# Earlier output copy, earlier first values and a score ring that runs across four heads

## The chip, the cores and the metric

The kernel runs on one core of one Trainium2 chip. The metric is the device time of one execution in microseconds (us); less is better. Three executions of the kernel before took 1312.82, 1315.09 and 1315.27 us.

## The reference

The input x is four sequences of 1024 tokens with 128 features, float32. Three residual steps follow each other, each on a layer-normalised x: half of a mixture-of-experts feed-forward, attention, and half of the same feed-forward again.

```
x = x + 0.5 * ffn(layernorm(x))          # 8 experts of width 256, top 2, silu gate
x = x + attention(layernorm(x))
x = x + 0.5 * ffn(layernorm(x))

attention: qkv = x @ qkv_w + qkv_b; 16 heads of 8; rotary on q and k
           weights = softmax(q @ k.T * 8**-0.5); out = (weights @ v) @ out_w + out_b
```

Batch times heads gives 64 independent heads, each with a score matrix of 1024 by 1024. This change touches only the attention over these heads.

## The kernel before, in words

All engines run hand-written instruction streams that meet at semaphores. The feed-forward stages are left as they are. The heads are handled one after the other, in a loop whose body holds four heads (u = 0 to 3), with the first four and the last four heads written out.

The scores of one head are computed twice on TensorE. Once with queries on the partitions, so that VectorE can take each query's maximum (`max_scores`, L866, and the reduction at L1243); and once with keys on the partitions, so that ScalarE can exponentiate them (`key_scores`, L895, and L662) and TensorE can multiply the exponentials with the values (`weigh_values`, L908). The maximum is split into three bf16 parts on GpSimd (L503 to L509), transposed on TensorE (`max_transpose`, L885), copied to SBUF by ScalarE (`mrow_copy`, L642) and brought by DMA (L360) into three extra rows of the query operand, so that the second score product comes out with the maximum already subtracted.

TensorE's order within head n is a loop over i = 0 to 15. In step i it issues one key-score matmul of head n (512 columns) and one max-score matmul of head n+2 (512 columns). After an odd i it issues one block of values: eight recorded matmuls for one block kb of 128 keys. Values run LAG = 2 blocks behind the scores, so after i = 1 and i = 3 the last two blocks (6 and 7) of head n-1 are done, and after i = 7, 9, 11, 13, 15 the blocks 1 to 5 of head n. Block 0 of head n stands after i = FIRST_VALUES = 6. The transposition of head n+1's maxima stands before i = MT_AT = 7. The values of a head add up in PSUM bank 7, which ScalarE copies out (`o_copy`, L650) after the exponential i = 3 of the next head; the copy waits until values block 7 is done, and values block 0 of the next head waits for the copy.

PSUM is cut thus: banks 0 to 2 are a ring for key scores and the transposed maxima; banks 3 to 6 are two pairs for the max scores; bank 7 holds the values' sum. A place of the ring is one bank in turn (place modulo 3). The ring has 18 places per head: sixteen scores, the transposition at place 7, and place 17, which is left empty so that the next head starts at bank 0 again. `place_before` names the work that used the same bank before, and `bank_free` makes TensorE wait for its reader on ScalarE. A max-score pair t (i = 2t and 2t+1) waits until VectorE has read pair t-2 (L865).

SyncE's queue issues, per head: the loads of Q and K of head n+3 (L353), the store of the copied output (L366) and the load of the maxima's rows (L360), each behind its semaphore.

Of the kernel before, what the change touches and what calls it, by code (L numbers as in the profile page):

```python
# [23 lines left out]
BF16 = mybir.dt.bfloat16  # L24
# [4 lines left out]
ACT = mybir.ActivationFunctionType  # L29
AX_X = mybir.AxisListType.X  # L30

P = 128
# [10 lines left out]
CH = 512  # L43
# [4 lines left out]
KB = T // P  # L48
PARTS = 3
# [4 lines left out]
ROWS = STACK + PARTS  # L54
# [4 lines left out]
PIECE = H * CH // P  # L59
QSLOTS = 4  # L60
LAG = 2
FIRST_VALUES = 2 * LAG + 2
PSLOTS = 8
HALVES = 2 * KB


MT_AT = 7
SCORE_BANKS = 3
PLACES = 18
SCORE_PLACE = [i + (i >= MT_AT) for i in range(HALVES)]  # L70
MT_BANK = MT_AT % SCORE_BANKS
FIRST_PAIRS = 3
W_OPS = 5
NEWTON = 3
# [2 lines left out]
def at_least(eng, sem, count):  # L77

    if isinstance(count, int) and count <= 0:
        return  # L80
    eng.wait_ge(sem, count)


def place_before(place, row):


    if place >= SCORE_BANKS:
        n, before = 0, place - SCORE_BANKS
    else:
        n, before = -1, place - SCORE_BANKS + PLACES  # L90
    if before == PLACES - 1 or (before == MT_AT and not row):
        before -= SCORE_BANKS
    if before == MT_AT:
        return n, None
    return n, SCORE_PLACE.index(before)


class Order:
# [32 lines left out]
def build(nc, x_in, qkv_w, qkv_b, v_b, out_w, out_b, wr_t, w1_in, w2_t, cos_t, sin_t, out):  # L131
# [4 lines left out]
    with ExitStack() as ctx:  # L136
        def sb(name, shape, dt=F32):
            return ctx.enter_context(nc.sbuf_tensor(name, shape, dt))

        def sem(name):  # L140
            return ctx.enter_context(nc.semaphore(name))
# [59 lines left out]
        K = [K_all[u // 2 * HALF:(u // 2 + 1) * HALF, u % 2, :] for u in range(QSLOTS)]  # L201
        probs = sb("probs", [P, PSLOTS, T])
# [6 lines left out]
        mparts = sb("mparts", [P, 2, PARTS, KB], BF16)  # L209
        mrow = sb("mrow", [PARTS * KB, 2, P], BF16)  # L210
# [7 lines left out]
        ps = ctx.enter_context(nc.psum_tensor("ps", [P, 8, 512], F32))  # L218
# [8 lines left out]
        wpsum = [ps[:, 4, :], mpsum_all]  # L227
        rpsum = ps[:, 7, 0:TPC * E].rearrange("p (t e) -> p t e", t=TPC)
        vpsum = ps[:, 7, :].rearrange("p (t h d) -> p t h d", t=TPC, h=H)
        score = [ps[:, SCORE_PLACE[i] % SCORE_BANKS, :] for i in range(HALVES)]  # L230
        maxps = [ps[:, SCORE_BANKS + 2 * s:SCORE_BANKS + 2 * s + 2, :] for s in range(2)]
        first_maxps = [ps[:, 2 * s:2 * s + 2, :] for s in range(FIRST_PAIRS)]
        mpsum = ps[0:PARTS * KB, MT_BANK, 0:P // 2].bitcast(BF16)
        opsum = ps[:, 7, 0:QW]


# [48 lines left out]
        mrow_ready = sem("mrow_ready")  # L285
# [252 lines left out]
        def _(sc):  # L538

            def xT_copy(p, k, bank=tpsum):  # L540
                sc.wait_ge(xT_in_psum, p + 1)

                at_least(sc, logits_in_psum, p - 1)
                nc.scalar.activation(xnT[:, k, :], bank, ACT.Copy).then_inc(xnT_ready, 1)
                at_least(sc, value_in_psum, 2 * E * (p - 1))
                nc.scalar.activation(x_hi[:, k, :], bank, ACT.Copy, scale=X_SCALE).then_inc(x_hi_ready, 1)
# [85 lines left out]
                hi_part(NCH - 1, w)  # L632
                mid_part(NCH - 1, w)

            def mrow_copy(r, u):
                n = QSLOTS * r + u
                sc.wait_ge(mT_in_psum, n + 1)

                if not (isinstance(r, int) and r == 0 and u < 2):
                    back = (u - 2) % QSLOTS  # L640
                    sc.wait_ge(mrow_loaded[back], 16 * (r + (1 if u >= 2 else 0)))
                nc.scalar.activation(mrow[:, u % 2, :], mpsum, ACT.Copy).then_inc(mrow_ready, 1)  # L642

            def o_copy(r, u):
                n = QSLOTS * r + u
                sc.wait_ge(probs_used, KB * (n + 1))

                if not (isinstance(r, int) and r == 0 and u < 2):
                    sc.wait_ge(ot_stored[u % 2], 16 * (2 * r + u // 2))
                nc.scalar.activation(ot[:, u % 2, :], opsum, ACT.Copy).then_inc(ot_ready, 1)  # L650

            def head(r, u, more=True, first=False):
                n = QSLOTS * r + u
                for i in range(HALVES):
                    kb, j = i // 2, i % 2
                    if i == MT_AT and more:
                        mrow_copy(r + (u + 1) // QSLOTS, (u + 1) % QSLOTS)
                    sc.wait_ge(scores_in_psum, HALVES * n + i + 1)
                    if j == 0:

                        at_least(sc, probs_used, KB * (n - 1) + kb + 1)
                    nc.scalar.activation(probs[:, kb % PSLOTS, j * CH:(j + 1) * CH], score[i],  # L662
                                         ACT.Exp, scale=SCALE).then_inc(probs_ready, 1)
                    if i == 3 and not first:
                        o_copy(r + (u - 1) // QSLOTS, (u - 1) % QSLOTS)
                    if i == 5 and not more:
                        xT_copy(NCH, 0, early_t)

            mrow_copy(0, 0)
            for u in range(QSLOTS):  # L670
                head(0, u, first=(u == 0))
            with sc.Fori(1, NH // QSLOTS - 1) as r:
# [11 lines left out]
        def _(pe):  # L684
# [171 lines left out]
            def operands(r, u):  # L856
                pe.wait_ge(head_loaded[u], 32 * (r + 1))

            def max_scores(r, u, i):

                t, half = i // 2, i % 2
                n = QSLOTS * r + u
                if half == 0:

                    pe.wait_ge(max_read, KB * n + t - 1)  # L865
                last = nc.tensor.matmul(maxps[t % 2][:, half, :], Q[u][0:STACK, t * P:(t + 1) * P],  # L866
                                        K[u][0:STACK, half * CH:(half + 1) * CH], start=True, stop=True)
                if half == 1:
                    last.then_inc(max_in_psum, 1)

            def bank_free(n, place, row):

                dn, i = place_before(place, row)
                if i is None:
                    pe.wait_ge(mrow_ready, n + dn + 2)
                else:
                    at_least(pe, probs_ready, HALVES * (n + dn) + i + 1)

            def max_transpose(r, u, first=False):

                n = QSLOTS * r + u
                pe.wait_ge(mparts_ready, n + 1)
                if not first:
                    bank_free(n - 1, MT_AT, True)
                nc.tensor.transpose(mpsum, mparts[:, u % 2, :, :].rearrange("p i t -> p (i t)"),  # L885
                                    identb[:]).then_inc(mT_in_psum, 1)

            def key_scores(r, u, i, row):

                n = QSLOTS * r + u  # L890
                kb, j = i // 2, i % 2
                if i == 0:
                    pe.wait_ge(mrow_loaded[u], 16 * (r + 1))
                bank_free(n, SCORE_PLACE[i], row)
                nc.tensor.matmul(score[i], K[u][0:ROWS, kb * P:(kb + 1) * P],  # L895
                                 Q[u][0:ROWS, j * CH:(j + 1) * CH], start=True, stop=True).then_inc(scores_in_psum, 1)

            def weigh_values(r, u, kb):
# [15 lines left out]
            pe.wait_ge(head_loaded[1], 32)  # L914
            for i in range(HALVES):
                if i == MT_AT:
                    max_transpose(0, 0, first=True)
                max_scores(0, 1, i)

            pe.wait_ge(v_ready, NCH)  # L920
# [2 lines left out]
            def head(r, u, maxes=True, row=True, first=False, early=None, ahead=True):  # L923
                for i in range(HALVES):
                    kb, j = i // 2, i % 2
                    if i == HALVES - 1 and ahead:
                        operands(r + (u + 3) // QSLOTS, (u + 3) % QSLOTS)
                    if i == MT_AT and row:
                        max_transpose(r + (u + 1) // QSLOTS, (u + 1) % QSLOTS)
                    key_scores(r, u, i, row)  # L930
                    if maxes:
                        max_scores(r + (u + 2) // QSLOTS, (u + 2) % QSLOTS, i)
                    if i == FIRST_VALUES:
                        weigh_values(r, u, 0)
                    elif j == 1 and kb > LAG:
                        weigh_values(r, u, kb - LAG)
                    elif j == 1 and kb < LAG and not first:
                        weigh_values(r + (u - 1) // QSLOTS, (u - 1) % QSLOTS, KB + kb - LAG)
                    if early == 0 and i == 5:

                        pe.wait_ge(max_read, KB * NH)
                        out_projection(0, early_t)
                    if early == 1 and i == 3:
                        x_transposes(NCH, 0, 0, early_t)
                    if early == 1 and i == 9:
                        router(NCH, 0, 0, early_r)
# [386 lines left out]
```

## Time and profile before

| what | value |
|---|---|
| runs | 1312.82, 1315.09, 1315.27 us (median 1315.09) |
| the profiled execution | 1314.48 us, of which the span from the first to the last instruction is 1312.4 us |
| TensorE matmul busy | 1275.5 us, 97% |
| VectorE busy | 1111.3 us, 85% |
| ScalarE busy | 803.4 us, 61% |
| GpSimd busy | 142.6 us, 11% |
| mean granted TensorE clock | 0.985 of full |

Matmuls overlap each other and the ends of their records are modelled, so a busy share of 97% does not mean that TensorE has no room. The attention over heads runs from about 384 us to 1011 us in the span. In this stretch VectorE and ScalarE are over 90% busy too, and what matters is the order of single instructions within one head.

### The profile page before, as it was taken

To read this page: it belongs to the slowest core of one execution; us is meant where nothing else is said; L and a number is where in the kernel's file an instruction comes from. 1 tells how busy PE (TensorE), PEld (TensorE's weight loads), DVE (VectorE), ACT (ScalarE), POOL (GpSimd) and SP (SyncE) were. 2 spreads that over 40 slices of the span, in tenths; PEclk is the share of its full clock that TensorE was granted. 3 is DMA by queue.
4 is the path that set the end of the run, shared out by engine and by line. 5 is a ranking of instruction groups with operands and counts; after the bars stand their busy time and mean duration, and the time that the engine had idled before them with its cause. 6 is when DMAs were issued, how large, how long until landed. Compare 5 with 4: busy or idle time off the path is not lost.

```text
span 1312.4 us, 32041 instructions
## 1 busy us (share of the span) xinstructions
PE 1275.5 (97%) x10240; PEld 620.6 (47%) x10240; DVE 1111.3 (85%) x2306; ACT 803.4 (61%) x1540; POOL 142.6 (11%) x450
## 2 busy tenths in 40 slices
PE   5999999999889999999999999999999999999998
PEld 3666666666522222222222222222223777767776
DVE  7888867887789999999999999999994777767775
ACT  4433333333239999999999999999997333233332
POOL 1020122111221111111111111111110000000000
PEclk9999999999969999999999999999998999999999
DMA  7010111011211110111101111110110101000000
GB/s 209 1 29 21 49 49 48 5 45 49 67 55 32 42 31 31 41 31 39 32 31 41 31 39 32 31 41 31 40 46 20 30 27 27 27 27 25 9 9 9
DMA packets 52265, 48.49 MB, mean 37 GB/s; under 512 B 10080, under 2 KB 44768, under 8 KB 52192
## 3 DMA queue, kind: packets, MB, share of 16 engines
q1 hardware_dynamic: 52192, 47.61, 12.6%
q8 instruction: 34, 0.56, 0.2%
q14 instruction: 39, 0.32, 0.1%
HBM read 23.86 MB, written 23.33 MB: 36 GB/s over the span
## 4 chain that ended last, share of the span: by engine, by line
PE 91%; DVE 6%; issue 2%; ACT 0%; DMA 0%; DVEq 0%; SPq 0%; ACTq 0%
PE ps L766 23%; PE ps L908 22%; PE ps L895 22%; PE ps L753 16%; PE ps L866 2%; PE ps L723 2%; DVE mx L1243 2%; PE ps L743 1%; DVE X L1100 1%; PE ps L687 1%; PE ps L730 1%; PE ps L760 1%; DVE act L1088 1%; DMA w<-w_t 0%; PE ps L705 0%
## 5 line engine op out<-in xcount | busy, mean ns | idle before, releaser
L1243 DVE TENSOR_REDUCE mx<-ps 128x1 f32<-128x1024 f32 x512 | 591.4, 1217 | 27.3 <-PE ps L866 21.3
L662 ACT ACTIVATE probs<-ps 128x512 f32<-128x512 f32 x1024 | 557.6, 603 | 57.9 <-PE ps L895 49.4
L591 ACT ACTIVATE sg<-ps,unscale 128x512 f32<-128x512 f32 x256 | 174.2, 689 | 306.5 <-PE ps L766 282.3
L866 PE MATMUL ps<-K,Q 48*128 48x512 bf16 x1008 | 329.7, 388 | 3.6 <-DVE mx L1243 3.0
L895 PE MATMUL ps<-Q,K 51*128 51x512 bf16 x1024 | 328.6, 386 | 1.4 <-ACT probs L662 0.7
L908 PE MATMUL ps<-probs,vh 128*32 128x256 f32 x4096 | 329.3, 394 | 0.0
L753 PEld LDWEIGHTS ps<-w,act 128*128 128x128 f32 x2048 | 247.9, 192 | 17.1
L753 PE MATMUL ps<-w,act 128*128 128x128 f32 x2048 | 249.0, 275 | 0.0
L1088 DVE SCALAR_TENSOR_TENSOR act<-ps,unscale,sg 128x512 f32<-128x512 f32 x256 | 183.4, 744 | 59.8 <-ACT sg L591 18.9
L766 PE MATMUL ps<-x_hi,w_hi 128*128 128x512 f16 x512 | 195.6, 382 | 9.4 <-DVE act L1088 6.2
L1100 DVE SCALAR_TENSOR_TENSOR X<-ps,rw,X 128x128 f32<-128x128 f32 (+1 forms) x512 | 143.8, 343 | 62.5 <-PE ps L753 61.9
L766 PE MATMUL ps<-x_lo,w_hi 128*128 128x512 f16 x512 | 195.4, 382 | 0.0
L766 PE MATMUL ps<-x_hi,w_lo 128*128 128x512 f16 x512 | 195.3, 381 | 0.0
L895 PEld LDWEIGHTS ps<-Q,K 51*128 51x128 bf16 x1024 | 73.2, 93 | 248.9 <-ACT probs L662 241.1
L908 PEld LDWEIGHTS ps<-probs,vh 128*32 128x32 f32 x4096 | 81.2, 108 | 176.3 <-ACT probs L662 131.6
L866 PEld LDWEIGHTS ps<-K,Q 48*128 48x128 bf16 x1008 | 72.2, 93 | 27.6 <-DVE mx L1243 26.6
L766 PEld LDWEIGHTS ps<-x_hi,w_hi 128*128 128x128 f16 x512 | 51.8, 101 | 63.0 <-DVE act L1088 11.9
L766 PEld LDWEIGHTS ps<-x_hi,w_lo 128*128 128x128 f16 x512 | 50.4, 98 | 61.4 <-issue 1.7
L766 PEld LDWEIGHTS ps<-x_lo,w_hi 128*128 128x128 f16 x512 | 50.3, 98 | 49.6 <-issue 5.5
L503 POOL TENSOR_SCALAR negm<-mx 128x8 f32<-128x8 f32 x64 | 15.1, 236 | 484.1 <-DVE mx L1243 484.1
L482 POOL TENSOR_TENSOR qf<-rot 128x512 f32<-128x512 f32 x16 | 20.4, 1272 | 258.6 <-DVE rot L1132 258.6
L581 ACT ACTIVATE tanh_gap<-gap 128x4 f32<-128x4 f32 x16 | 3.3, 206 | 52.4 <-DVE gap L1057 52.4
(84 smaller groups left out, 608.9 us busy)
## 6 DMA issues: line engine op xcount, KB each, us to landing
o_parts<-ot SPq DMA_DIRECT2D x64, 128.0 KB, 1.9
q_stack<-parts SPq DMA_DIRECT2D x48, 128.0 KB, 2.3
k_stack<-parts SPq DMA_DIRECT2D x48, 128.0 KB, 2.3
Q<-q_stack SPq DMA_DIRECT2D x64, 96.0 KB, 2.3
K<-k_stack SPq DMA_DIRECT2D x64, 96.0 KB, 2.3
probs<-w_in SPq DMA_DIRECT2D x8, 256.0 KB, 4.5
att<-o_parts SPq DMA_DIRECT2D x16, 128.0 KB, 2.6
rden<-rdens SPq DMA_DIRECT2D x16, 128.0 KB, 2.5
```

The lines of the kernel that those rows point to most:

```text
L482: nc.gpsimd.tensor_tensor(qf[:, w, :], rot[:, w, 0, :], rot[:, w, 1, :], ALU.add).then_inc(rot_sum, 1)
L591: nc.scalar.activation(sg[:, j, :], hid[2 * j], ACT.Silu, scale=unscale[:, e, 2 + j:3 + j]).then_inc(silu_done, 1)
L662: nc.scalar.activation(probs[:, kb % PSLOTS, j * CH:(j + 1) * CH], score[i], ACT.Exp, scale=SCALE).then_inc(probs_ready, 1)
L723: last = nc.tensor.matmul(bank, wqkv[:, 2 * w + i, :], x2T[:], start=True, stop=True)
L753: last = nc.tensor.matmul(ypsum[s][:, t, :], act[:, s, j, t * P:(t + 1) * P], w2[:, e, j, :], start=(j == 0), stop=(j == 1))
L766: last = nc.tensor.matmul(bank, w[:, e, at:at + P], x[:, k, :], start=(n == 0), stop=(n == 2))
L866: last = nc.tensor.matmul(maxps[t % 2][:, half, :], Q[u][0:STACK, t * P:(t + 1) * P], K[u][0:STACK, half * CH:(half + 1) * CH], start=True ...
L895: nc.tensor.matmul(score[i], K[u][0:ROWS, kb * P:(kb + 1) * P], Q[u][0:ROWS, j * CH:(j + 1) * CH], start=True, stop=True).then_inc(scores_ ...
L908: last = nc.tensor.matmul(opsum[VW * c:VW * (c + 1), :], vh[:, u % 2, kb, :], probs[:, kb % PSLOTS, c * QW:(c + 1) * QW], start=(kb == 0), ...
L1088: nc.vector.scalar_tensor_tensor(out=act[:, e % 2, j, :], in0=hid[2 * j + 1], scalar=unscale[:, e, j:j + 1], in1=sg[:, j, :], op0=ALU.mult ...
L1100: last = nc.vector.scalar_tensor_tensor(out=xt, in0=ypsum[e % 2][:, t, :], scalar=rw[:, k, t, e:e + 1], in1=xt, op0=ALU.mult, op1=ALU.add)
L1243: nc.vector.tensor_reduce(mx[:, u % 2, t:t + 1], pair.rearrange("p a b -> p (a b)"), AX_X, ALU.max).then_inc(max_read, 1)
```

## The change

The empty place at the end of each head goes. The ring now has 17 places per head (HEAD_PLACES), so four heads take 68 places, and one empty place follows them: 69 places, which divides by 3. The bank of a score now depends on u, the head's place among the four. The transposition moves from before i = 7 to before i = 6. Values block 0 moves from after i = 6 to after i = 5. ScalarE's copy of the last head's output moves from behind the exponential i = 3 to behind i = 2. The number of instructions stays as it is.

```diff
-FIRST_VALUES = 2 * LAG + 2
+FIRST_VALUES = 2 * LAG + 1
...
-MT_AT = 7
+MT_AT = 6
 SCORE_BANKS = 3
-PLACES = 18
-SCORE_PLACE = [i + (i >= MT_AT) for i in range(HALVES)]
-MT_BANK = MT_AT % SCORE_BANKS
+HEAD_PLACES = HALVES + 1
+PLACES = QSLOTS * HEAD_PLACES + 1
...
+def score_place(u, i):
+    return HEAD_PLACES * u + i + (i >= MT_AT)
+
+def bank_of(place):
+    return place % SCORE_BANKS
+
+def mt_bank(u):
+    return bank_of(HEAD_PLACES * u + MT_AT)
+
+def place_before(u, place, row):
+    n, before = 0, place - SCORE_BANKS
+    if before < 0:
+        n, before = -QSLOTS, before + PLACES
+    if before == PLACES - 1 or (before == HEAD_PLACES * u + MT_AT and not row):
         before -= SCORE_BANKS
-    if before == MT_AT:
+    n += before // HEAD_PLACES - u
+    at = before % HEAD_PLACES
+    if at == MT_AT:
         return n, None
-    return n, SCORE_PLACE.index(before)
+    return n, at - (at > MT_AT)
...
-        score = [ps[:, SCORE_PLACE[i] % SCORE_BANKS, :] for i in range(HALVES)]
+        score = [[ps[:, bank_of(score_place(u, i)), :] for i in range(HALVES)] for u in range(QSLOTS)]
...
-                    if i == 3 and not first:
+                    if i == 2 and not first:
                         o_copy(r + (u - 1) // QSLOTS, (u - 1) % QSLOTS)
```

## Rows read from the trace of the kernel before

**Rows 1.** The page's costliest groups; columns as xcount, busy us, mean ns, idle before.

```profile
L1243 DVE TENSOR_REDUCE mx<-ps 128x1 f32<-128x1024 f32 x512 | 591.4, 1217 | 27.3 <-PE ps L866 21.3
L908 PE MATMUL ps<-probs,vh 128*32 128x256 f32 x4096 | 329.3, 394 | 0.0
```

**Rows 2.** Waits from 600 to 800 us: waiter, awaited, total us, times, longest.

```profile
ACT probs L662 <- PE ps L895: 13.8, 42, 0.4
DVE mx L1243 <- PE ps L866: 6.5, 21, 0.3
PEld ps L866 <- DVE mx L1243: 5.1, 21, 0.2
```

**Rows 3.** Timeline, 700 to 711 us: start, duration, engine, line, operation, count, idle before.

```profile
700.25 9.34 DVE L1243 TENSOR_REDUCE mx<-ps 128x1 f32<-128x1024 f32 x8 [0.31 <-PE ps L866]
...
702.90 0.39 PE L895 MATMUL ps<-Q,K 51*128 51x512 bf16 x1
...
704.00 0.39 PE L895 MATMUL ps<-Q,K 51*128 51x512 bf16 x1
...
705.65 0.39 PE L895 MATMUL ps<-Q,K 51*128 51x512 bf16 x1
...
705.97 0.64 PE L908 MATMUL ps<-probs,vh 128*32 128x256 f32 x8
...
706.54 0.39 PE L895 MATMUL ps<-Q,K 51*128 51x512 bf16 x1
...
707.04 1.09 ACT L662 ACTIVATE probs<-ps 128x512 f32<-128x512 f32 x2 [0.28 <-PE ps L895]
...
707.07 0.64 PE L908 MATMUL ps<-probs,vh 128*32 128x256 f32 x8
...
707.53 0.20 POOL L509 TENSOR_TENSOR mparts<-negm,mparts 128x8 bf16<-128x8 f32 x1
...
707.93 0.34 SPq L353 DMA_DIRECT2D Q<-q_stack  x1
...
708.01 0.39 ACT L650 ACTIVATE ot<-ps 128x256 f32<-128x256 f32 x1
...
708.27 1.60 ACT L662 ACTIVATE probs<-ps 128x512 f32<-128x512 f32 x3
...
708.51 0.39 PE L866 MATMUL ps<-K,Q 48*128 48x512 bf16 x1
...
708.83 0.64 PE L908 MATMUL ps<-probs,vh 128*32 128x256 f32 x8
...
709.29 0.22 PE L885 MATMUL ps<-identb,mparts 128*24 128x128 bf16 x1
...
709.44 0.39 PE L895 MATMUL ps<-Q,K 51*128 51x512 bf16 x1
...
709.90 1.23 DVE L1243 TENSOR_REDUCE mx<-ps 128x1 f32<-128x1024 f32 x1 [0.31 <-PE ps L866]
...
710.33 0.39 PE L895 MATMUL ps<-Q,K 51*128 51x512 bf16 x1
```

**Rows 4.** Timeline of ScalarE alone, in half microseconds around 707.5 and 709.

```profile
707.53 0.59 ACT L662 ACTIVATE probs<-ps 128x512 f32<-128x512 f32 x1
...
708.75 1.12 ACT L662 ACTIVATE probs<-ps 128x512 f32<-128x512 f32 x2
```

**Rows 5.** Timeline of TensorE from 703.9 us: the second half of a values block.

```profile
703.67 0.40 PE L908 MATMUL ps<-probs,vh 128*32 128x256 f32 x4
```

**Rows 6.** Timeline, 398.4 to 401 us, in the heads written out before the loop.

```profile
398.45 0.64 PE L908 MATMUL ps<-probs,vh 128*32 128x256 f32 x8
...
399.15 0.32 SPq L353 DMA_DIRECT2D Q<-q_stack  x1
```

**Rows 7.** Timeline, 364 to 412 us, before the first head's exponentials.

```profile
379.36 0.28 PE L885 MATMUL ps<-identb,mparts 128*24 128x128 bf16 x1
...
379.58 1.50 PE L866 MATMUL ps<-K,Q 48*128 48x512 bf16 x3
...
380.22 9.48 DVE L1243 TENSOR_REDUCE mx<-ps 128x1 f32<-128x1024 f32 x8 [0.23 <-PE ps L866]
```

More of the change, by code:

```diff
@@ L81, in at_least @@
     eng.wait_ge(sem, count)
[L84 to L91, printed above, removed]
+def score_place(u, i):
[9 more added lines that the diff above has]
+    if before == PLACES - 1 or (before == HEAD_PLACES * u + MT_AT and not row):
         before -= SCORE_BANKS
-    if before == MT_AT:
+    n += before // HEAD_PLACES - u
+    at = before % HEAD_PLACES
+    if at == MT_AT:
         return n, None
-    return n, SCORE_PLACE.index(before)
+    return n, at - (at > MT_AT)
 class Order:
@@ L229, in build @@
         vpsum = ps[:, 7, :].rearrange("p (t h d) -> p t h d", t=TPC, h=H)
-        score = [ps[:, SCORE_PLACE[i] % SCORE_BANKS, :] for i in range(HALVES)]
+        score = [[ps[:, bank_of(score_place(u, i)), :] for i in range(HALVES)] for u in range(QSLOTS)]
         maxps = [ps[:, SCORE_BANKS + 2 * s:SCORE_BANKS + 2 * s + 2, :] for s in range(2)]
         first_maxps = [ps[:, 2 * s:2 * s + 2, :] for s in range(FIRST_PAIRS)]
-        mpsum = ps[0:PARTS * KB, MT_BANK, 0:P // 2].bitcast(BF16)
+        mpsum = [ps[0:PARTS * KB, mt_bank(u), 0:P // 2].bitcast(BF16) for u in range(QSLOTS)]
         opsum = ps[:, 7, 0:QW]
@@ L633, in _, with mrow_copy @@
                 mid_part(NCH - 1, w)
-            def mrow_copy(r, u):
+            def mrow_copy(r, u, beside):
                 n = QSLOTS * r + u
@@ L641, in mrow_copy @@
                     sc.wait_ge(mrow_loaded[back], 16 * (r + (1 if u >= 2 else 0)))
-                nc.scalar.activation(mrow[:, u % 2, :], mpsum, ACT.Copy).then_inc(mrow_ready, 1)
+                nc.scalar.activation(mrow[:, u % 2, :], mpsum[beside], ACT.Copy).then_inc(mrow_ready, 1)
             def o_copy(r, u):
@@ L656, in head @@
                     if i == MT_AT and more:
-                        mrow_copy(r + (u + 1) // QSLOTS, (u + 1) % QSLOTS)
+                        mrow_copy(r + (u + 1) // QSLOTS, (u + 1) % QSLOTS, u)
                     sc.wait_ge(scores_in_psum, HALVES * n + i + 1)
@@ L661, in head @@
                         at_least(sc, probs_used, KB * (n - 1) + kb + 1)
-                    nc.scalar.activation(probs[:, kb % PSLOTS, j * CH:(j + 1) * CH], score[i],
+                    nc.scalar.activation(probs[:, kb % PSLOTS, j * CH:(j + 1) * CH], score[u][i],
                                          ACT.Exp, scale=SCALE).then_inc(probs_ready, 1)
-                    if i == 3 and not first:
+                    if i == 2 and not first:
                         o_copy(r + (u - 1) // QSLOTS, (u - 1) % QSLOTS)
@@ L667, in head @@
                         xT_copy(NCH, 0, early_t)
-            mrow_copy(0, 0)
+            mrow_copy(0, 0, 0)
             for u in range(QSLOTS):
@@ L869, in max_scores, with bank_free @@
                     last.then_inc(max_in_psum, 1)
-            def bank_free(n, place, row):
-                dn, i = place_before(place, row)
+            def bank_free(n, u, place, row):
+                dn, i = place_before(u, place, row)
                 if i is None:
@@ L877, in bank_free, with max_transpose @@
                     at_least(pe, probs_ready, HALVES * (n + dn) + i + 1)
-            def max_transpose(r, u, first=False):
+            def max_transpose(r, u, beside, first=False):
                 n = QSLOTS * r + u
@@ L883, in max_transpose @@
                 if not first:
-                    bank_free(n - 1, MT_AT, True)
-                nc.tensor.transpose(mpsum, mparts[:, u % 2, :, :].rearrange("p i t -> p (i t)"),
+                    bank_free(n - 1, beside, HEAD_PLACES * beside + MT_AT, True)
+                nc.tensor.transpose(mpsum[beside], mparts[:, u % 2, :, :].rearrange("p i t -> p (i t)"),
                                     identb[:]).then_inc(mT_in_psum, 1)
@@ L893, in key_scores @@
                     pe.wait_ge(mrow_loaded[u], 16 * (r + 1))
-                bank_free(n, SCORE_PLACE[i], row)
-                nc.tensor.matmul(score[i], K[u][0:ROWS, kb * P:(kb + 1) * P],
+                bank_free(n, u, score_place(u, i), row)
+                nc.tensor.matmul(score[u][i], K[u][0:ROWS, kb * P:(kb + 1) * P],
                                  Q[u][0:ROWS, j * CH:(j + 1) * CH], start=True, stop=True).then_inc(scores_in_psum, 1)
@@ L916, in _ @@
                 if i == MT_AT:
-                    max_transpose(0, 0, first=True)
+                    max_transpose(0, 0, 0, first=True)
                 max_scores(0, 1, i)
@@ L928, in head @@
                     if i == MT_AT and row:
-                        max_transpose(r + (u + 1) // QSLOTS, (u + 1) % QSLOTS)
+                        max_transpose(r + (u + 1) // QSLOTS, (u + 1) % QSLOTS, u)
                     key_scores(r, u, i, row)
```

## The prediction, made before the result was known

> **What bounds the kernel now.** The page comes first. It shows TensorE busy almost throughout, but matmul ends are modelled, and VectorE's largest group is the reduction of the maxima: 512 of them, 1217 ns each, with 21.3 us of idle time that the max scores end [rows 1]. The waits of the steady stretch come second: from 600 to 800 us ScalarE waits 42 times for key scores, VectorE waits 21 times 0.31 us for max scores, and TensorE's max scores wait 21 times for VectorE [rows 2]. There are 21 heads in these 200 us, so each head has two stalls of ScalarE and one of VectorE. The third view is the timeline of one head, which says where they are. I write K0 to K15 for the key-score matmuls of a head, E0 to E15 for their exponentials, M0 to M15 for the max scores, R0 to R7 for the reductions, V0 to V7 for the values blocks, T for the transposition, and o for ScalarE's copy of the output.
>
> I count from K2 of a head, at 706.54 [rows 3]. E2 starts at 0.50 (707.04), V7 of the last head at 0.53, E3 at 0.99 [rows 4], o at 1.47, E4 at 1.73, E5 at 2.21 [rows 4], M6 at 1.97, V0 at 2.29, T at 2.75, K7 with M7 at 2.90, R3 at 3.36 and K8 at 3.79 [rows 3].
>
> Two cycles of equal length close here. One goes through VectorE: eight reductions start 1.161 us apart ((9.34 - 1.215) / 7), the end of R1 releases M6, then V0 (0.32), T (0.46), M7 (0.15), R3 (0.46). The 0.31 us stall stands before R3, as V0 and T lie between M6 and M7. The other goes through ScalarE: E2, E3, o, E4, E5 run back to back, E5's end releases K7's bank (2.21 + 0.63 + 0.06 = 2.90), then K7 to K8 0.89, K8 to K14 3.32 (three pairs of steps with their values; the last takes 1.10, 702.90 to 704.00), K14 to K2 of the next head 2.54. That is 2.90 + 0.89 + 3.32 + 2.54 = 9.65 us a head. Either cycle alone holds the head at 9.65.
>
> **The ring.** Place 17 is empty now, so K0 waits for E14 and K1 for E15; K1 stands 1.65 behind K14 (704.00 to 705.65), V6 follows 0.32 later and K2 0.57 after that [rows 3]. With 17 places K0 waits for E13, K1 for E14, K2 for E15, all done in time, and two pairs of 1.105 bring K2 2.21 after K14. That saves 0.33 us at each boundary that has no empty place. There are 63 boundaries, 15 of them (u = 3 to u = 0) keep it: 48 * 0.33 = 15.8 us off the ScalarE cycle. From below the saving is nothing, if M2 is held in its place: M2 needs R7's end, which by K7 + 0.46 + 4 * 1.161 + 1.215 + 0.04 comes at K7 + 6.36, and K2 stands at K7 + 6.42. It fits by 0.06 us, so I take the full 0.33.
>
> **V0 and T.** Their costs do not change, only their places. M6 and M7 now follow each other, so VectorE gets its third pair 0.61 us sooner after R1 (0.46 + 0.15), more than the stall of 0.31. The cycle through VectorE falls to the 8 * 1.161 = 9.29 us of the reductions. T needs E3's end and GpSimd's parts; the latter are ready at 707.73, 1.19 on my count [rows 3], while T comes at about 2.2. V0 waits for o. T's copy by ScalarE still comes behind E5, and its DMA load is issued no later than now, over 4 us ahead of the next K0; the loads of Q and K on the same queue hang on V7 and move with it, and the output's store is issued behind them. None of these is late. What this removes from VectorE is worth nothing unless the ScalarE cycle shrinks too.
>
> **The copy o.** It moves between E2 and E3. ScalarE would reach it at 0.98, but it needs V7, which starts only at 0.53. Before, E3 covered this wait. How long V7 takes to reach ScalarE has no row of its own, since o never waited in the steady heads. Its last four matmuls start 0.24 behind the first four (703.67 in a block that starts 703.43, which is the 0.57 ahead of K14 at 704.00) [rows 5], and a matmul of 0.39 us, as they are [rows 1], releases an exponential 0.50 after its start (K2 to E2) [rows 3]. That gives 0.74. So o starts at 0.53 + 0.74 = 1.27 instead of 0.98: a wait of 0.29 us. Queued behind o on ScalarE are E3, E4 and E5, and TensorE waits for E4 and E5 to free the banks of K6 and K7; K7 then stands at 2.90 + 0.29 = 3.19. Bounds: V7's array time is over when the next K starts, 0.57 behind it (705.97 to 706.54), so at least 1.10, a wait of 0.12. From above, SyncE's load that waits for the same V7 is issued 0.86 behind its start in the loop (707.07 to 707.93) [rows 3] and 0.70 in the heads written out [rows 6]; 0.86 makes the wait 0.41. The same kind of row, a matmul seen by ScalarE, stands nearest, so I take 0.74.
>
> The page's recorded end of V7 is 0.64 behind its start [rows 3]. The Trainium skill (Perfetto Trace Analysis, "Per-instruction lifecycle") says that TensorE's recorded end is estimated from the instruction's size, and that the write's acknowledgement and the semaphore's way to the other engines lie behind it. The trace agrees: K2's record ends 0.39 behind its start and E2 starts at 0.50. This rule speaks against the change, since o would otherwise wait only 0.19.
>
> V0, with its bank freed at 1.27 + 0.39 + 0.05 = 1.71, then T and K6 at 2.3, are not late: K6 waits for E4's end at 2.7 anyway.
>
> **The sum.** With o's wait each head without the empty place takes 9.65 - 0.33 + 0.29 = 9.61, one with it 9.94. VectorE's 9.29 lies below both. The last two heads have no max scores and their own gaps; 61 copies pay: 61 * 0.29 = 17.7. Against 15.8 saved this is +1.9 us. At the start of the stage the transposition waits for GpSimd, and M6 now stands behind it instead of before: T at 379.36 was followed 0.22 later by M7 and 0.64 after that by R3 at 380.22 [rows 7]; one more matmul between them puts R3 later by 0.2 to 0.4 us, once. I add 0.2. Total +2.1 us on the profiled execution's 1314.48 (span 1312.4 and 2.1 around it) is 1316.6; it lies 0.6 under the median of the runs, so on the median it is 1317.2. I forecast 1317, that is no change that a measurement of this kernel could tell (0.2%, 2.6 us), two gains and a loss of nearly equal size.
>
> **The rivals.**
> Slower: the copy becomes the wait that takes the place of the one removed. From a reaction of 0.77 us on the loss is over 2.6 us (61 * 0.32 = 19.5, less 15.8, and 0.2 is 3.9). At SyncE's 0.86 it is 61 * 0.41 = 25.0, so +9.4 and 1324. For it: in the loop the copy waits on two semaphores with computed values, as SyncE's load does, and the written-out heads show 0.16 less. Against it: E2 has such waits too and starts after 0.50.
> Faster: V7 reaches ScalarE early. If the recorded end of 0.64 held, the wait is 0.19: 61 * 0.19 = 11.6, -4.0 us, 1311. At the bound of 0.57 it is 7.3, -8.3 us, 1307. For it: both ends are modelled. Against it: the 0.11 between K2's recorded end and E2.
> The ring saves nothing: M2, 0.06 from being late, is held by VectorE, or another wait keeps K2 where it is. Then only the copy's cost is left, 17.7 + 0.2: 1333. Against it: the reductions run back to back and R7's time is fixed by K7, which moves the whole head.
> A head at VectorE's 9.29 throughout would give 61 * 0.36 = 22 us less, but the order of V7, o, E3 rules it out, as V7's array time alone is longer than ScalarE's way to o.
>
> **How the numbers follow.** My forecast has 0.44, of which 0.34 lies within 0.2%, 0.07 above and 0.03 below. The faster rival has 0.22 (0.18 beyond 0.2%), the slower one 0.26, the ring without effect 0.08. Faster is 0.21, same 0.38, slower 0.41. The range runs from 1307, the early bound of V7, to 1325, just past SyncE's bound, and leaves out the dead ring and some of the tails. The likeliest case's own range is 1313 to 1320.
>
> **What would show it.** In the profile after: ScalarE has an idle time before L650 in each head, some 0.15 to 0.2 us behind E2's end, ended by L908; a start of L650 0.74 behind V7's start confirms the step, 0.64 or 0.86 are the rivals. K2 stands 2.21 behind K14 in three heads of four and 2.54 in the fourth. Heads take 9.61 and 9.94 in turn. VectorE still stalls before R3, 0.3 us and more, and the wait of L866 for L1243 goes from M6. If heads take 9.4 or less the copy did not wait, and I am wrong there; if all four take over 9.7, the ring's saving is what failed.

## The result: some 2 to 3 us slower, two large effects that nearly cancel

| | median of the runs | ratio to before, 95% interval |
|---|---|---|
| before | 1314.66 us (10 runs) | |
| changed | 1317.78 us (10 runs) | 1.0024 [1.0016, 1.0032] |
| changed, measured again later | 1315.88 us (11 runs; before beside it 1314.25) | 1.0013 [1.0004, 1.0022] |

The forecast was 1317. The change costs 1.6 to 3.1 us, 0.13 to 0.24%, which straddles the bound of 0.2% that the prediction called no change. The two measurements of one kernel differ by 1.9 us, so less than that is read from traces here and not from medians.

The first view of the changed kernel's trace is the timeline of one head, u = 0 of the loop. Its rows answer to [rows 3] and [rows 4]; L664 is the output copy (o), L676 the exponentials, L909 the key scores, L880 the max scores, L922 the values and L1257 the reductions. The letters K, E, M, R, V and T are those of the prediction, and o is the copy.

```profile
699.81 0.39 PE L909 MATMUL ps<-Q,K 51*128 51x512 bf16 x1
...
700.31 0.60 ACT L676 ACTIVATE probs<-ps 128x512 f32<-128x512 f32 x1 [0.28 <-PE ps L909]
...
700.35 0.64 PE L922 MATMUL ps<-probs,vh 128*32 128x256 f32 x8
...
701.14 0.38 ACT L664 ACTIVATE ot<-ps 128x256 f32<-128x256 f32 x1 [0.23 <-PE ps L922]
...
701.42 1.57 ACT L676 ACTIVATE probs<-ps 128x512 f32<-128x512 f32 x3
...
703.05 0.39 PE L909 MATMUL ps<-Q,K 51*128 51x512 bf16 x1
...
703.51 8.01 DVE L1257 TENSOR_REDUCE mx<-ps 128x1 f32<-128x1024 f32 x7 [0.64 <-PE ps L880]
```

The reader is to see the new wait: ScalarE ends E2 at 700.91 and stands idle 0.23 us until values block 7 releases the copy at 701.14, 0.79 us behind that block's start (700.35). E3, E4 and E5 follow at 701.42, and K7, held by E5's bank, comes at 703.05, which is 3.24 on the count from K2 (699.81) instead of 2.90. VectorE's stall before R3 grew from 0.31 to 0.64 us, since M7 goes with K7.

The second view is the copy in the four heads behind that one (ScalarE's timeline, L664), which with the 701.14 above gives the length of each head, and a row of the kernel before (L650), where the copy of the head ahead of it stands at 708.01 [rows 3].

```profile
710.80 0.38 ACT L664 ACTIVATE ot<-ps 128x256 f32<-128x256 f32 x1 [0.23 <-PE ps L922]
720.38 0.38 ACT L664 ACTIVATE ot<-ps 128x256 f32<-128x256 f32 x1
730.03 0.38 ACT L664 ACTIVATE ot<-ps 128x256 f32<-128x256 f32 x1 [0.23 <-PE ps L922]
740.01 0.38 ACT L664 ACTIVATE ot<-ps 128x256 f32<-128x256 f32 x1 [0.23 <-PE ps L922]
```

```profile
717.66 0.39 ACT L650 ACTIVATE ot<-ps 128x256 f32<-128x256 f32 x1
```

Before, every head of the loop takes 9.65 us. Now four heads take 9.66, 9.58, 9.65 and 9.98, together 38.87 instead of 38.60. This pattern repeats through the loop and costs 0.27 us per four heads.

The profiled executions were 1314.48 and 1315.66 us, only 1.2 apart. The windows of the last head say why. The columns are the stretch and its length, busy time of TensorE, its weight loads, VectorE, ScalarE and GpSimd, granted clock, DMA share and GB/s. The kernel before:

```profile
1004.70:1011.10 6.40, 6.33 (x45) 1.56 (x44) 1.81 (x15) 3.13 (x7) 0.00 (x0) 0.56 0.00 0
```

The changed kernel:

```profile
1007.40:1012.30 4.90, 4.81 (x51) 1.60 (x50) 2.10 (x19) 3.37 (x8) 0.00 (x0) 1.00 0.00 0
```

In the execution of before, TensorE was granted about half its clock (1.2 of 2.4 GHz) for most of this stretch, and full clock in that of the changed kernel. The last copy came 12.80 us behind the last but one before and 9.83 after. These 3 us hide most of what the loop lost. They come and go between executions of the changed kernel; the second profiles, at the end of the experiments, come back to whether they do in the kernel before.

### The profile page after: what moved, and what is told of

It reads as the page before. It is cut to its first block, busy times and chain, and to the rows that moved or that the text cites. A ratio compares the mean times of both kernels' runs of the same rounds, so it can differ in the third digit from the quotient of the medians.

```text
span 1313.7 us, 32055 instructions
## 1 busy us (share of the span) xinstructions
PE 1254.6 (96%) x10240; PEld 613.8 (47%) x10240; DVE 1108.1 (84%) x2306; ACT 812.1 (62%) x1540; POOL 141.8 (11%) x450
## 4 chain that ended last, share of the span: by engine, by line
PE 86%; DVE 4%; issue 4%; ACT 4%; POOL 1%; ACTq 0%; DMA 0%; DVEq 0%; SPq 0%; POOLq 0%
PE ps L780 23%; PE ps L909 21%; PE ps L922 20%; PE ps L767 16%; ACT probs L676 3%; PE ps L737 2%; PE ps L757 1%; DVE X L1114 1%; PE ps L701 1%; PE ps L880 1%; DVE act L1102 1%; PE ps L774 1%; DVE mx L1257 1%; PE ps L744 0%; DMA w<-w_t 0%
## 5 line engine op out<-in xcount | busy, mean ns | idle before, releaser
L1257 DVE TENSOR_REDUCE mx<-ps 128x1 f32<-128x1024 f32 x512 | 587.5, 1217 | 36.3 <-PE ps L880 34.9
L676 ACT ACTIVATE probs<-ps 128x512 f32<-128x512 f32 x1024 | 555.5, 596 | 37.8 <-PE ps L909 30.4
L909 PE MATMUL ps<-Q,K 51*128 51x512 bf16 x1024 | 324.4, 385 | 16.1 <-ACT probs L676 12.3
L922 PE MATMUL ps<-probs,vh 128*32 128x256 f32 x4096 | 328.7, 393 | 6.3 <-ACT ot L664 3.3
L880 PE MATMUL ps<-K,Q 48*128 48x512 bf16 x1008 | 322.1, 389 | 3.1 <-DVE mx L1257 3.0
L909 PEld LDWEIGHTS ps<-Q,K 51*128 51x128 bf16 x1024 | 71.8, 93 | 235.2 <-ACT probs L676 204.4
L922 PEld LDWEIGHTS ps<-probs,vh 128*32 128x32 f32 x4096 | 82.3, 108 | 203.3 <-ACT probs L676 147.6
L880 PEld LDWEIGHTS ps<-K,Q 48*128 48x128 bf16 x1008 | 71.0, 93 | 10.3 <-DVE mx L1257 9.4
```

What stands on the lines that cost most here:

```text
L909: nc.tensor.matmul(score[u][i], K[u][0:ROWS, kb * P:(kb + 1) * P], Q[u][0:ROWS, j * CH:(j + 1) * CH], start=True, stop=True).then_inc(scor ...
L922: last = nc.tensor.matmul(opsum[VW * c:VW * (c + 1), :], vh[:, u % 2, kb, :], probs[:, kb % PSLOTS, c * QW:(c + 1) * QW], start=(kb == 0), ...
L1257: nc.vector.tensor_reduce(mx[:, u % 2, t:t + 1], pair.rearrange("p a b -> p (a b)"), AX_X, ALU.max).then_inc(max_read, 1)
```

## The experiments

Four heads of the loop are the yardstick: the starts of the output copy, read from ScalarE's timeline. Each kernel's median is of 4 to 10 executions, and the ratio is to the kernel before, run beside it (1314.2 to 1314.3 us). The clock of the last head moves single executions by up to 3 us, so effects are read from the four heads, which ran at full clock in every profile; the loop repeats them 14 times (56 heads).

| kernel | ring | T, V0 | copy behind | four heads, us | sum | median, ratio to before [95%] |
|---|---|---|---|---|---|---|
| before | 18 | 7, 6 | E3 | 9.65, 9.65, 9.65, 9.65 | 38.60 | |
| ring_only | 69 | 7, 6 | E3 | 9.33, 9.45, 9.45, 9.77 | 38.00 | 1303.67, 0.9927 [0.9911, 0.9944] |
| order_only | 18 | 6, 5 | E3 | 9.66, 9.64, 9.64, 9.64 | 38.58 | 1312.21, 0.9989 [0.9980, 0.9999] |
| copy_only | 18 | 7, 6 | E2 | 10.00, 9.92, 9.99, 10.01 | 39.92 | 1330.83, 1.0128 [1.0111, 1.0145] |
| ring_and_order | 69 | 6, 5 | E3 | 9.34, 9.32, 9.33, 9.64 | 37.63 | 1298.40, 0.9883 [0.9858, 0.9908] |
| ring_and_copy | 69 | 7, 6 | E2 | 9.69, 9.59, 9.68, 10.01 | 38.97 | 1315.95, 1.0017 [1.0008, 1.0027] |
| changed | 69 | 6, 5 | E2 | 9.66, 9.58, 9.65, 9.98 | 38.87 | see above |
| after_swapped | 69 | 6, 5 | E2 | 9.57, 9.57, 9.57, 9.90 | 38.61 | 1312.18, 0.9990 [0.9980, 1.0000] |
| before_waits | 18 | 7, 6 | E3 | 9.57, 9.56, 9.57, 9.57 | 38.27 | 1310.39, 0.9965 [0.9953, 0.9978] |
| ring_order_waits | 69 | 6, 5 | E3 | 9.27, 9.24, 9.24, 9.49 | 37.24 | 1293.51, 0.9844 [0.9828, 0.9861] |

**The ring alone.** The changed kernel with three lines as before:

```diff
-FIRST_VALUES = 2 * LAG + 1
+FIRST_VALUES = 2 * LAG + 2
-MT_AT = 6
+MT_AT = 7
-                    if i == 2 and not first:
+                    if i == 3 and not first:
```

> The ring of 69 places alone; transposition before i = 7, first values after i = 6 and output copy behind the exponential i = 3, as in the kernel before. My theory (two cycles of 9.65 us a head, one through VectorE with the first values and the transposition between M6 and M7, one through ScalarE with the empty place): the ScalarE cycle shrinks by 0.33 us in three heads of four, the VectorE cycle does not, so heads stay at 9.65 and the time is that of before within 2 us (about 1315). Rival, the ScalarE cycle alone sets the head: heads of 9.32, 9.32, 9.32 and 9.65 us, about 15 us less, 1299.

It took 1303.67 us, 10.6 less than before. The loop gives 14 * 0.60 = 8.4 of that, and the last head of the profile was at full clock. My theory, that it gains nothing, fell here: the VectorE cycle is not 9.65 us long. VectorE's timeline in this kernel has these rows for a head with no empty place ahead of it and one with:

```profile
705.21 9.14 DVE L1257 TENSOR_REDUCE mx<-ps 128x1 f32<-128x1024 f32 x8 [0.31 <-PE ps L880]
...
724.11 9.34 DVE L1257 TENSOR_REDUCE mx<-ps 128x1 f32<-128x1024 f32 x8 [0.31 <-PE ps L880]
```

Eight reductions need 9.14 us when nothing holds them, and with the stall of 0.31 the cycle is 9.45, which is what two of the four heads take. The 9.34 of [rows 3] held a wait inside. Narrow windows of VectorE's timeline in the kernel before show it, with a max score on TensorE (L866):

```profile
704.78 1.21 DVE L1243 TENSOR_REDUCE mx<-ps 128x1 f32<-128x1024 f32 x1
...
706.10 1.23 DVE L1243 TENSOR_REDUCE mx<-ps 128x1 f32<-128x1024 f32 x1
...
705.65 0.39 PE L866 MATMUL ps<-K,Q 48*128 48x512 bf16 x1
```

R7 starts at 704.78 and R0 at 706.10, 1.32 later; with the ring alone the reductions follow each other by 1.13 (709.75, 710.88, 712.01). R0 needs M1, which was issued at 705.65 right behind K1, and K1 was what the empty place held. So the empty place lay in both cycles.

**The order alone.** The kernel before with `MT_AT = 6` and `FIRST_VALUES = 2 * LAG + 1`.

> The ring of 18 places with its empty place in every head; only the transposition goes to before i = 6 and the first values to after i = 5; output copy behind the exponential i = 3. My theory: the VectorE cycle falls to 9.3 us but the ScalarE cycle stays at 9.65, so heads stay at 9.65 and the time is that of before within 2 us. The first values must wait for the copy (released at 1.91 on the count from K2 instead of the natural 1.64), which the wait for the bank of K6 hides. Rival, the VectorE cycle alone sets the head: heads of 9.3 to 9.4 us, 1295 to 1300. Rival, first values waiting for the copy delay K7: over 9.65, 1320 or more.

The loop's heads stay at 9.64 to 9.66 us. The VectorE cycle is shorter and nothing comes of it while the ScalarE cycle holds the head. The median is 2 us lower, with the interval just short of 1; its profile's last head was at full clock, and no head of its loop is more than 0.01 us shorter, so in the loop the order itself gained nothing that the trace shows.

**The changed kernel without the early copy.**

```diff
-                    if i == 2 and not first:
+                    if i == 3 and not first:
```

> The changed kernel with one part undone: the output copy stands behind the exponential i = 3 as before. My theory: both cycles shrink and the copy does not wait, so heads take 9.32, 9.32, 9.32 and 9.65 us, mean 9.40, some 15 us less than before: 1299 to 1301. Then the moved copy is what the change lost. Rival, the ring saves nothing in its place because M2 or another wait holds K2: heads stay at 9.58 to 9.65 and the time at 1312 to 1315. Rival, first values that wait for the copy cost what the early copy costs: about 1317.

As expected: 1298.40 us, with three heads at 9.32 to 9.34 and one at 9.64. ScalarE's timeline shows the copy straight behind E3 with no idle time:

```profile
698.62 2.18 ACT L676 ACTIVATE probs<-ps 128x512 f32<-128x512 f32 x4
...
700.69 0.39 ACT L664 ACTIVATE ot<-ps 128x256 f32<-128x256 f32 x1
...
700.96 1.11 ACT L676 ACTIVATE probs<-ps 128x512 f32<-128x512 f32 x2
```

One line separates this from the changed kernel. It costs 1.24 us per four heads, 17.4 us in the loop, and 17.5 or 19.4 us between the medians, by which median of the changed kernel one takes. That the first values wait for the later copy does no harm.

**The early copy alone.** The kernel before with `i == 3` turned into `i == 2` for the copy.

> The kernel before with one line changed: the output copy behind the exponential i = 2. Ring of 18 places, transposition before i = 7, first values after i = 6. My theory: the copy starts 0.79 us behind values block 7 instead of 0.47 behind E2's start as ScalarE could, and delays E3 to E5 and with them K7 by 0.33 to 0.35 us: heads of 10.0 us, 61 * 0.34 = 21 us more than before, 1335. Rival, there is slack behind E5 that takes the wait up: heads of 9.65 and 1315.

1330.83 us, 16.5 over before. The heads take the expected 10.0 us; ScalarE's timeline shows the wait (values block 7 started at 706.52):

```profile
706.49 0.60 ACT L662 ACTIVATE probs<-ps 128x512 f32<-128x512 f32 x1 [0.27 <-PE ps L895]
...
707.32 0.38 ACT L650 ACTIVATE ot<-ps 128x256 f32<-128x256 f32 x1 [0.23 <-PE ps L908]
```

The copy starts 0.80 behind the values, and no slack behind E5 takes it up. The expected 21 us was high by 4.5. The loop has 56 heads and not 61, which makes 14 * 1.32 = 18.5 us, and this profile's last head was at full clock, so that the last four took 2.5 us less than before's (39.96 against 42.51).

**Ring and early copy without the new order.** The changed kernel with `MT_AT = 7` and `FIRST_VALUES = 2 * LAG + 2`.

> The changed kernel without its new order on TensorE: ring of 69 places and the copy behind i = 2, but the transposition before i = 7 and the first values after i = 6. My theory: the wait of the copy and the ring set the head at 9.66, 9.58, 9.66 and 9.99 us, and the VectorE cycle, 9.45 as the ring alone showed it, lies below that, so the new order is worth nothing beside the early copy: within 1.5 us of the changed kernel, 1317.8. Rival, the new order is what keeps the changed kernel from being slower (VectorE's stall adds to the copy's wait): heads of 9.8 and over, 1325 or more.

Four heads take 38.97 us against the changed kernel's 38.87: the new order is worth 0.1 us per four heads beside the early copy, 1.4 us over the loop, and nothing that the medians can tell (1315.95 against 1315.88 and 1317.78). Without the early copy it is worth 38.00 - 37.63 = 0.37 per four, and 5.3 us between the medians.

**The copy's two waits exchanged.** In the changed kernel one head of four has no recorded idle time before its copy. There values block 7 started at 719.67 and the copy at 720.38, 0.71 later and not 0.79. Both its waits compare with values worked out in the loop, but in that head (u = 2) the second value is the same as in the head before.

```diff
-                sc.wait_ge(probs_used, KB * (n + 1))
                 if not (isinstance(r, int) and r == 0 and u < 2):
                     sc.wait_ge(ot_stored[u % 2], 16 * (2 * r + u // 2))
+                sc.wait_ge(probs_used, KB * (n + 1))
```

> The changed kernel; only the two waits of the output copy are exchanged: it waits first for the old store of its buffer, then for values block 7. In the changed kernel the copy starts 0.79 us behind the start of values block 7 in three heads of the loop and 0.71 in the one (u = 2) whose second wait needs a value that was computed before. My theory: the 0.08 us is ScalarE's sequencer working out the second wait's value after the first wait has passed; exchanged, it starts 0.71 behind in all heads, three heads of four are 0.08 shorter, 3.6 us less than the changed kernel: about 1314. Rival, the 0.08 comes from something else (ScalarE's queue, the semaphore): no change, 1317.8.

The heads are 9.57, 9.57, 9.57 and 9.90, 0.26 less per four. Values and copy in ScalarE's and TensorE's timeline (L921 and L663 here):

```profile
708.06 0.64 PE L921 MATMUL ps<-probs,vh 128*32 128x256 f32 x8
...
708.77 0.38 ACT L663 ACTIVATE ot<-ps 128x256 f32<-128x256 f32 x1
```

0.71 us, in every head of the loop. The median of 1312.18 lies 3.7 and 5.6 under the two of the changed kernel; the loop gives 14 * 0.26 = 3.6.

In the heads written out behind the loop, whose waits compare with constants, the exchange did the opposite. There the changed kernel's copy starts 0.71 behind the values, and here 0.76 to 0.78:

```profile
978.42 0.64 PE L921 MATMUL ps<-probs,vh 128*32 128x256 f32 x8
...
979.18 0.38 ACT L663 ACTIVATE ot<-ps 128x256 f32<-128x256 f32 x1 [0.28 <-PE ps L921]
```

**The exchange in the kernel before**, for the copy and for the even exponentials, which have two waits too:

```diff
-                    sc.wait_ge(scores_in_psum, HALVES * n + i + 1)
                     if j == 0:
                         at_least(sc, probs_used, KB * (n - 1) + kb + 1)
+                    sc.wait_ge(scores_in_psum, HALVES * n + i + 1)
```

> The kernel before, with ScalarE's two waits exchanged wherever it has two: the exponentials wait first for the values block that frees their buffer, then for the scores; the output copy first for the old store, then for the values. My theory: a value worked out between two waits costs 0.08 us once the first has passed; E2 then starts 0.42 behind K2 instead of 0.50, as in the heads written out, and each head is 0.08 shorter, 9.57: 61 * 0.08 = 4.9 us less than before, 1309.5. Rival, the 0.08 belongs to the loop in another way (the queue, the fetch): no change, 1314.5.

1310.39 us, 4.0 less. The loop's heads are 9.57, and K2 and E2 stand 0.43 apart instead of 0.50:

```profile
704.75 0.39 PE L893 MATMUL ps<-Q,K 51*128 51x512 bf16 x1
...
705.18 1.08 ACT L660 ACTIVATE probs<-ps 128x512 f32<-128x512 f32 x2 [0.26 <-PE ps L893]
```

In the heads written out E2 went the other way again, from 0.42 behind K2 (967.20 to 967.62 in the kernel before) to 0.49 (963.19 to 963.68 here).

**Everything that helped.** Ring, order, late copy and exchanged waits.

> Ring of 69 places, transposition before i = 6, first values after i = 5, output copy behind i = 3, and ScalarE's two waits exchanged as in before_waits. My theory: heads of 9.24, 9.24, 9.24 and 9.56 us, as the heads written out ahead of the loop took in ring_and_order (9.25, 9.24, 9.56), 0.08 less each: about 4.8 us less than ring_and_order's 1298.4, 1293.6. Rival, VectorE's reductions (8 of 1.132 to 1.161 us, 9.06 to 9.29) become the bound: 9.29 a head and 1296.

1293.51 us, ratio 0.9844 to before: 21 us faster than the kernel before and 22 to 24 faster than the changed one. The loop's heads are 9.24 to 9.27, and 9.49 where the empty place is left (9.56 was expected); the heads written out ahead of it take 9.30, where without the exchange they took 9.24 and 9.25. VectorE's floor of 9.06 (8 * 1.132) does not bind yet.

**Second profiles of both kernels**, unchanged.

> The changed kernel once more, for its spread and a second profile. In the first profiles the last head ran at half TensorE clock for some 6.6 us in the kernel before (12.8 us from the last but one output copy to the last) and at full clock in the changed kernel (9.8 us), which hides 3 us of the 4.1 us that the loop's heads show. My theory: the loop costs 4.1 us in every profile and the tail's clock comes and goes with the execution; the median is 3 us over before, and a profile with the half clock in the tail would read about 1318.5. Rival, the changed kernel never has the half clock there: this profile again has a last head of 9.8 us.

> The kernel before once more, for a second profile. My theory: heads of 9.65 us in the loop again; the last head either 12.8 us (half clock) or 10 us, and the profiled time 1314.5 or 1311.5 accordingly; it comes and goes with the execution. Rival, the half clock in the tail belongs to the kernel before: 12.8 us again.

The second profile of the changed kernel was 1317.17 us, that of before 1314.49 (median of its 11 executions 1313.97). The loop repeats to the hundredth. The last head of the changed kernel ran at half clock this time (12.78 us):

```profile
1008.00:1014.00 6.00, 5.87 (x40) 1.44 (x36) 1.20 (x8) 2.36 (x7) 0.00 (x0) 0.53 0.00 0
```

So the changed kernel has either course: two executions of it differ in the clock of the last head, while TensorE's wait for ScalarE ahead of it is the same, 0.20 us, and stands 3.48 us behind the last copy but one in both (at 1004.64 here and at 1005.93 in the first profile).

Whether the kernel before ever has the full clock there is open, and what is on record speaks rather against it. Both of its profiles had the half clock. Of the 66 executions of it whose mean granted clock was noted, none was above 0.987, and none of all 76 took less than 1312.36 us, where the full clock in the tail should give about 1311.3 (an estimate, 3 us under the median). Of the changed kernel's 21 executions five had 0.988, with 1314.8 to 1315.7 us, and ten had 0.985 or less, with 1317.2 to 1319.0. So the change may also have made the full clock in the tail more likely, and its medians may look better for it. Nothing here tests that.

With the same clock in the tail the account closes. Starts of the copy, changed less before: up to the fourth copy -0.60 us, over the next 56 heads +3.79 (544.09 against 540.30), over the last four -0.47. The sum is +2.7, and the spans differ by 2.7 (1315.2 and 1312.5).

## Why the prediction was right, point by point

**The ring's saving.** Right in size. K14 to K2 is 2.22 us where no empty place stands between (707.26 to 709.48 in the changed kernel), forecast was 2.21, and copy_only (39.92 per four) against ring_and_copy (38.97) gives 0.95, three times 0.32; forecast was 0.33. That M2 would hold K2 did not happen.

**The copy's wait.** The mechanism was right, and its size 0.05 us short. It starts 0.79 us behind values block 7, forecast was 0.74, from the time between K2 and E2. That row was the right kind to take, for its 0.50 itself holds the 0.07 of a second wait. The whole step from 37.63 to 38.87 per four heads is 0.31 a head, where 0.29 was forecast. The recorded end of 0.64 would have given too little: the copy starts 0.07 us (0.71 with the waits exchanged) to 0.15 us behind it. The Trainium skill (Perfetto Trace Analysis, "Per-instruction lifecycle") says that TensorE's recorded end is an estimate and that the semaphore comes after it, and this trace agrees.

**Heads of 9.61 and 9.94.** They are 9.65, 9.66 and 9.98, and one of 9.58. I had not foreseen that one head in four escapes the 0.08 us.

**The VectorE cycle.** This is the step that failed: "Either cycle alone holds the head at 9.65." The ring alone gained 8.4 us in the loop and 10.6 between the medians, because eight reductions need 9.14 us and not 9.34, and R0 waited for M1 behind K1. The forecast did not hang on it, since with the early copy the ScalarE cycle is the longer one in any case. A forecast of the ring alone would have been wrong by 10 us. The merged row (9.34 x8, with an idle time given for its start alone) hid a gap of 0.19 us within.

**V0 and T.** Their new places cost nothing (38.87 with them against 38.97 without, and 37.63 against 38.00 with the late copy). VectorE's stall stayed, as said, and even grew, since M7 waits for E5 through K7.

**The start.** Forecast was 0.2 us more once, and the step itself came out at that. R3 of these first pairs started 3.80 us behind R0 before (376.42 to 380.22, with 0.23 idle ahead of it [rows 7]) and 4.00 in the changed kernel:

```profile
375.99 3.58 DVE L1257 TENSOR_REDUCE mx<-ps 128x1 f32<-128x1024 f32 x3
...
379.99 9.48 DVE L1257 TENSOR_REDUCE mx<-ps 128x1 f32<-128x1024 f32 x8 [0.42 <-PE ps L880]
```

In the totals it drowns. In the pair of profiles with like clock the fourth copy comes 0.6 us earlier, and in the first profile 0.9 later. In that first one the first head's exponentials came in pairs 1.98 us apart until 395.81, and from 390 to 395 us the granted clock was 0.50, where it was 0.74 in before and 0.76 in the second profile.

**The sum, and luck.** Forecast was +2.1; measured are +2.7 at like clock and +3.1 and +1.6 between medians. Part of this closeness is luck. By the prediction's own terms the loop's 56 heads should cost 2.4 us (14 * (4 * 0.29 - 3 * 0.33)), and they cost 3.8. What lies outside them should have given back 0.3, and it gave back 1.1. With the measured waits of 0.34 in three heads and 0.26 in the fourth the prediction's sum would have read +3.9 (61 * 0.32 - 15.8 + 0.2). I gave 0.38 to no change and 0.41 to slower, and the result lies on the bound between them.

## What to carry to other kernels

An instruction that waits for another engine's last result is best put behind work that covers the whole way of that result, which here is longer than the recorded block (0.71 to 0.79 us against 0.64). One place too early cost 17.4 us in this loop, more than the 13.6 that the ring and the order had gained there. When two cycles seem equally long, look for a wait they share, such as a held matmul whose neighbour in the queue feeds the other engine, before calling each of them a bound. Where a merged row of "busy" instructions sets a bound, read the starts one by one, as gaps below 0.2 us hide in it. And of two waits in a row in a hardware loop, try the one that is met last at the end; where the waits compared with constants, that order was the slower one here.

## What the runs showed of the hardware

In a hardware loop, ScalarE's reaction to a semaphore is 0.07 to 0.08 us later when a second wait with a computed value stands behind the one that is met last: 0.79 against 0.71 us for the copy, 0.50 against 0.43 for E2. Exchanging the two took it away in the loop, in all three kernels where it was tried. In the heads written out, where both waits compare with constants, the same exchange made it 0.05 to 0.07 us later instead: 0.71 to 0.76 or more for the copy, 0.42 to 0.49 for E2. That in the loop it is the sequencer working out the second value is my reading; no record shows the step, and it does not say why constants turn the effect round.

The granted TensorE clock of the last attention head is 0.53 to 0.56 in some executions and 1.00 in others of the same program. Ahead of it TensorE waits for ScalarE in both kinds, 0.18 and 0.52 us in before (at 1000.17 and 1001.64) and 0.20 us in both executions of the changed kernel. What decides was not settled. Of the ten kernels profiled, before_waits and after_swapped had the half clock there too (12.57 and 12.54 us from the last copy but one to the last), and the other six profiled once had the full clock (9.7 to 10.1). It moves the end of the stage by 3 us, as much as the change under study.
